# PSUM banks of an attention stage: one ring of seven, or four for row maxima and three for scores, with the maximum unit ahead of the scores on TensorE

## The chip, the cores and the metric

The program runs on one core of a Trainium2 chip. The metric is the device time of one execution in microseconds (us), the median of several. A core has TensorE (matrix products, which land in PSUM), VectorE (DVE in the profile), ScalarE (ACT), GpSimd (POOL) and SyncE (SP), each with its own instruction stream, tied together by semaphores. PSUM has eight banks of 128 x 512 fp32.

## The reference

The input x is 4 x 1024 x 128. Three sublayers are added to it: half a mixture of experts, attention, and half the same mixture again.

```python
x = x + 0.5 * _L0_ffn_ref(_layernorm(x, axis=-1), ...)   # 8 experts, top 2, 128 -> 512 -> 128
x = x + _L0_attn_ref(_layernorm(x, axis=-1), W_qkv, W_o)
x = x + 0.5 * _L0_ffn_ref(_layernorm(x, axis=-1), ...)

# attention: B, N, F, H = 4, 1024, 128, 16; DH = 8; queries, keys and values are one projection
qkv = (x @ W_qkv.T).reshape(b, n, H, DH).transpose(0, 2, 1, 3)
score = softmax(einsum('bhif,bhjf->bhij', qkv, qkv) / SQRT_D, axis=-1)
attn = einsum('bhij,bhjf->bihf', score, qkv)
out = attn.reshape(b, n, F) @ W_o.T
```

The softmax subtracts each row's own maximum, so every score is needed twice: once for the maximum, once for the exponential.

## The kernel before

The stages follow each other: routing, the experts of the first mixture, attention, the experts of the second, the last sums. The change touches attention alone.

Attention works on teams of four heads (NTEAM = 16 teams over four batches), each in two halves of 512 queries. Two kinds of products are made of the same operands:

- **Maximum units.** Unit n is two matmuls side by side in the array (rows 0 to 61 and 64 to 125), each 128 queries x 512 keys, into two PSUM banks (`tensor_row_max`, lines 2247 and 2248). VectorE reduces both banks to row maxima (`vector_row_max`): in one instruction over 1024 elements where the banks are neighbours (line 1970), in two over 512 where the ring wraps (line 1975). There are 512 units. When 16 are done, a "place" chore carries the maxima into the operands of the score products.
- **Score slots.** A slot is one matmul, 128 keys x 512 queries, into one bank; slots come in pairs (`tensor_scores`, lines 2264 and 2268), again side by side. ScalarE takes the exponential of each bank into `att_probs` (line 1456). There are 1024 slots, so 512 pairs. Four slots (two pairs) are a unit for the value products.

After each pair from the third on TensorE runs four value products (`tensor_values`, line 2286) of the unit before: part 0 with the first pair of a unit, part 1 with the second. Part 0 waits until ScalarE has emptied the last slot of that earlier unit, which is the second slot of the pair just before:

```python
if part == 0:
    ...
    TE.wait_ge(*att_bank.emptied(("score", UNIT * (n + 1) - 1)))
```

Below, a pair whose values are part 0 is called an **even pair**, one with part 1 an **odd pair**. For each half-team a "finish" chore copies the value bank out (line 1471) and turns it back through PSUM (line 2309), and further chores (prepare, rows, route) do the layernorm and projection of the next batch and the routing of the last mixture. They are handed out to fixed slots by the list `chores`, and stand behind the value products on each engine.

Everything in attention but the value bank shares seven PSUM banks. `Ring` deals them out in one order, that of the `plan` calls: the pair's two scores, its maximum unit, its chores. What takes a bank waits for whoever held it seven places earlier. TensorE takes its instructions in the order of the program: scores, maximum unit, values, chores. The first 26 maximum units (MAX_FIRST) are run before the first scores, so the unit beside pair k is number k + 26, and the last 26 pairs have none.

Of the kernel before, what the change touches and what calls it, by code (L numbers as in the profile page):

```python
# [9 lines left out]
ALU = mybir.AluOpType  # L10
ACT = mybir.ActivationFunctionType
AX = mybir.AxisListType


class Tally:


    def __init__(self, sem):
        self.sem, self.value = sem, 0
# [35 lines left out]
class Ring:  # L55
# [1 line left out]

    def __init__(self, banks, filled, by_act, maxed, reduced):  # L60
        self.banks = banks
        self.filled, self.by_act, self.maxed, self.reduced = filled, by_act, maxed, reduced
        self.at, self.number, self.holders = {}, {}, []
        self.count = {1: 0, 2: 0}
# [6 lines left out]
        self.number[name] = (size, self.count[size])  # L71

    def bank(self, name, k=0):
        return (self.at[name] + k) % self.banks

    def full(self, name):
        size, n = self.number[name]
# [13 lines left out]
def build_macaron(nc, x, w_qkv, w_o, ln_g, ln_b, router_w, eg, eb, w1, b1, w2, b2, wo, bo, out):  # L91
# [69 lines left out]
    PAIR = 2  # L161
# [15 lines left out]
    V, G, S, TE, Q = nc.vector, nc.gpsimd, nc.scalar, nc.tensor, nc.sync  # L177

    stack = ExitStack()
    with stack:  # L180
# [3 lines left out]
        def semaphore(name):  # L184
            return stack.enter_context(nc.semaphore(name))
# [46 lines left out]
        class RouteSet:  # L232


            def __init__(self, k, owner):
                def buf(name, shape, dt=F32):
                    return sbuf(f"{name}{k}", shape, dt, owner)

                self.stats = buf("stats", [P, BT, 6])
                self.mean_var = buf("mean_var", [P, BT, 2])  # L240
                self.shifted = buf("shifted", [P, BT])
                self.rstd = buf("rstd", [P, BT])
                self.xf = buf("xf", [P, BT, F])
                self.xf_t = buf("xf_t", [P, N])
                self.rows = buf("rows", [P, BT, TOPK, ROW])
                self.logits = buf("logits", [P, BT, E])
                self.others = buf("others", [P, BT, E])
                self.equal = buf("equal", [P, BT, E])
                self.foremost = buf("foremost", [P, BT])
                self.is_top = buf("is_top", [P, TOPK, BT, E])  # L250
                self.picked = buf("picked", [P, TOPK, BT, E])
                self.top = buf("top", [P, TOPK, BT])
                self.ratio = buf("ratio", [P, BT])
                self.chosen = buf("chosen", [P, BT, E], BF16)
                self.tallies = buf("tallies", [P, 2, E, BT + 1])
                self.counts = buf("counts", [P, E, BT + 1])
                self.place = buf("place", [P, BT, E])
                self.place_f = buf("place_f", [P, TOPK, BT])
                self.place_i = buf("place_i", [P, TOPK, BT], I32)
                self.by_dve = semaphore(f"route_dve{k}")  # L260
                self.by_pool = semaphore(f"route_pool{k}")
                self.by_act = semaphore(f"route_act{k}")
                self.rows_out = [semaphore(f"rows_out{k}_{j}") for j in range(TOPK)]
# [7 lines left out]
        psum = stack.enter_context(nc.psum_tensor("psum", [P, 8, 512], F32))  # L271
        bank = [psum[:, i, :] for i in range(8)]
# [5 lines left out]
        first = ExitStack()  # L278
# [26 lines left out]
        class Mixture:  # L305


            def __init__(self, k, beside):
                mixing = ExitStack()
                if beside:  # L310
# [138 lines left out]

        route_bank = [Banks([bank[b]], semaphore(f"route_full{b}"), semaphore(f"route_emptied{b}"))  # L450
                      for b in range(B)]
        att_bank = Ring(7, semaphore("bank_full"), semaphore("bank_emptied"), maxed, reduced)


        side_bank = Banks([value_bank], semaphore("side_full"), semaphore("side_emptied"))
# [134 lines left out]

        def max_banks(n):

            return [att_bank.bank(("max", n), k) for k in range(PAIR)]

        PLACINGS = 2 * NTEAM

# [165 lines left out]


        for n in range(MAX_FIRST):
            att_bank.plan(("max", n), 2)
            if n == HALF_UNITS + 1:
                for chore in first_chores:
                    plan_banks(*chore)
        for slot in range(0, NSCORES, 2):
            att_bank.plan(("score", slot))  # L770
            att_bank.plan(("score", slot + 1))
            for n in max_units(slot + 1):
                att_bank.plan(("max", n), 2)
            for chore in chores[slot] + chores[slot + 1]:
                plan_banks(*chore)
        for slot in HEAD + TAIL:
# [1187 lines left out]
        def vector_row_max(n):  # L1964
            i, g, p, t, keys = max_of(n)
            h = 2 * i + g
            V.wait_ge(maxed, n + 1)
            low, high = max_banks(n)
            if high == low + 1:
                last = V.tensor_reduce(out=neg_part[:, h % 2, keys, p::PAIR, t], in_=psum[:, low:high + 1, :],  # L1970
                                       axis=AX.X, op=ALU.max, negate=True)
            else:

                for k, where in enumerate((low, high)):
                    last = V.tensor_reduce(out=neg_part[:, h % 2, keys, PAIR * k + p, t:t + 1], in_=bank[where],  # L1975
                                           axis=AX.X, op=ALU.max, negate=True)
            last.then_inc(reduced, 1)
            if n % HALF_UNITS == HALF_UNITS - 1:
                V.wait_ge(reduced, n + 1)
                if h >= 2:  # L1980
                    V.wait_ge(*att_bank.full(("place", h - 2)))
                V.tensor_tensor(neg_max[:, h % 2, :], neg_part[:, h % 2, 0, :, :].rearrange("p j t -> p (j t)"),
                                neg_part[:, h % 2, 1, :, :].rearrange("p j t -> p (j t)"),
                                ALU.min).then_inc(max_whole, 1)
# [229 lines left out]
        def tensor_attention():  # L2214
            TE.wait_ge(weighed, BLOCKS)
            TE.wait_ge(combined, HC * BLOCKS)
            TE.wait_ge(turn_copied, BLOCKS)
            for n in range(MAX_FIRST):
                tensor_row_max(n)
                if n == HALF_UNITS + 1:  # L2220
                    for chore in first_chores:
                        tensor_chore(*chore)
            for slot in range(0, NSCORES, 2):
                tensor_scores(slot)
                for n in max_units(slot + 1):
                    tensor_row_max(n)
                if slot >= UNIT:
                    tensor_values(slot // UNIT - 1, slot % UNIT // 2)
                for chore in chores[slot] + chores[slot + 1]:
                    tensor_chore(*chore)  # L2230
            for part in range(2):
                tensor_values(NSCORES // UNIT - 1, part)

        def tensor_row_max(n):
            i, g, p, t, keys = max_of(n)
            s = i % OPERANDS
            if n == i * 2 * HALF_UNITS:
                if i < OPERANDS:
                    TE.wait_ge(max_rows_set, i + 1)
                TE.wait_ge(lefts_in[s], lefts_before(i))  # L2240
                TE.wait_ge(rights_in[s], rights_before(i))
            for emptied in att_bank.empty_before(("max", n)):
                TE.wait_ge(*emptied)
            low, high = max_banks(n)
            q = slice((g * HT + t) * P, (g * HT + t + 1) * P)
            k = slice(keys * HALF, (keys + 1) * HALF)
            TE.matmul(bank[low], left[s][PRODUCTS[0], p, q], right[s][PRODUCTS[0], p, k], start=True, stop=True)  # L2247
            TE.matmul(bank[high], left[s][PRODUCTS[1], p, q], right[s][PRODUCTS[1], p, k],  # L2248
                      start=True, stop=True).then_inc(maxed, 1)

        def tensor_scores(slot):

            i, at = divmod(slot, TURN)
            u, j = divmod(at, UNIT)
            half, kt = divmod(u, BT)
            s, p = i % OPERANDS, j // 2
            if kt == 0 and j == 0:
                TE.wait_ge(max_in[s], 16 * 2 * (placed_before(2 * i + half) + 1))
            low, high = ring_bank(("score", slot)), ring_bank(("score", slot + 1))
            k = slice(kt * P, (kt + 1) * P)  # L2260
            q = slice(half * HALF, (half + 1) * HALF)
            for emptied in att_bank.empty_before(("score", slot)):
                TE.wait_ge(*emptied)
            TE.matmul(low, left[s][WITH_MAX[0], p, k], right[s][WITH_MAX[0], p, q],  # L2264
                      start=True, stop=True).then_inc(att_bank.filled, 1)
            for emptied in att_bank.empty_before(("score", slot + 1)):
                TE.wait_ge(*emptied)
            TE.matmul(high, left[s][WITH_MAX[1], p, k], right[s][WITH_MAX[1], p, q],  # L2268
                      start=True, stop=True).then_inc(att_bank.filled, 1)
# [120 lines left out]
```

## Time and profile before

| | |
|---|---|
| time, median of 3 runs | 1316.57 us (1316.5 to 1319.73) |
| the profiled execution: time, span | 1308.1 us, 1306.4 us |
| scores, from the first to the last exponential | 364 to 1060 us |
| TensorE, VectorE, ScalarE busy, of the span | 88%, 86%, 68% |
| mean granted TensorE clock | 0.978 |

The busy share of TensorE comes from modelled ends of pipelined matmuls, so starts are the better reading: the distance from one start to the next is the pace. Exponentials and reductions overlap their neighbours by about 0.1 us, so a mean duration is longer than the step from one to the next.

### The profile page before, as it was taken

To read this page: it belongs to the slowest core of one execution; us is meant where nothing else is said; L and a number is where in the kernel's file an instruction comes from. 1 tells how busy PE (TensorE), PEld (TensorE's weight loads), DVE (VectorE), ACT (ScalarE), POOL (GpSimd) and SP (SyncE) were. 2 spreads that over 40 slices of the span, in tenths; PEclk is the share of its full clock that TensorE was granted. 3 is DMA by queue.
4 is the path that set the end of the run, shared out by engine and by line. 5 is a ranking of instruction groups with operands and counts; after the bars stand their busy time and mean duration, and the time that the engine had idled before them with its cause. 6 is when DMAs were issued, how large, how long until landed. Compare 5 with 4: busy or idle time off the path is not lost.

```text
span 1306.4 us, 27214 instructions
## 1 busy us (share of the span) xinstructions
PE 1150.1 (88%) x9031; PEld 630.4 (48%) x9031; DVE 1126.8 (86%) x2337; ACT 887.6 (68%) x1879; POOL 482.2 (37%) x545
## 2 busy tenths in 40 slices
PE   3847999888589999999999999999998889999993
PEld 2746888777123223223323223233322258788882
DVE  7877888877899999989998999999999368988885
ACT  1223555555168999898888888898887965455651
POOL 3873547334113000324235313333333117543232
PEclk9999999999679999999999999999999999999997
DMA  8124665564010200002001010001000503554654
GB/s 277 50 70 171 215 212 187 206 215 134 29 50 19 67 6 15 18 18 63 5 27 37 11 32 19 18 26 28 18 5 24 181 31 138 191 204 181 247 199 139
DMA packets 58617, 123.55 MB, mean 95 GB/s; under 512 B 12352, under 2 KB 33826, under 8 KB 58448
## 3 DMA queue, kind: packets, MB, share of 16 engines
q1 hardware_dynamic: 49488, 103.83, 23.1%
q0 software_dynamic: 8704, 16.93, 4.1%
q8 instruction: 75, 1.23, 0.4%
q10 hardware_dynamic: 288, 1.05, 0.2%
q14 instruction: 62, 0.51, 0.1%
HBM read 36.66 MB, written 23.88 MB: 46 GB/s over the span
## 4 chain that ended last, share of the span: by engine, by line
PE 56%; DVE 25%; issue 5%; POOL 5%; ACT 5%; DMA 3%; SPq 1%; DVEq 0%; POOLq 0%; ACTq 0%
PE psum L2286 14%; DVE att_neg_part L1970 12%; PE psum L2264 8%; PE psum L2200 8%; PE psum L2188 7%; PE psum L2190 7%; PE psum L2247 5%; POOL rows_dram L1263 4%; DVE att_neg_part L1975 2%; DMA ffn_block_rows<-rows_dram 2%; DVE ffn_x2c L1911 2%; DVE stats L1604 2%; ACT att_probs L1456 2%; DVE ffn_hidden L1922 1%; PE psum L2309 1%
## 5 line engine op out<-in xcount | busy, mean ns | idle before, releaser
L1456 ACT ACTIVATE att_probs<-psum 128x512 f32<-128x512 f32 x1024 | 554.9, 599 | 59.3 <-PE psum L2268 31.2
L1970 DVE TENSOR_REDUCE att_neg_part<-psum 128x2 f32<-128x1024 f32 x443 | 519.1, 1216 | 33.3 <-PE psum L2248 31.6
L2286 PE MATMUL psum<-att_probs,att_values 128*16 128x256 f32 x4096 | 322.1, 386 | 12.4 <-ACT att_o_t L1471 7.7
L1424 ACT ACTIVATE ffn_silu<-ffn_x2c,ffn_rec 128x256 f32<-128x256 f32 (+1 forms) x320 | 154.6, 487 | 170.1 <-DVE ffn_x2c L1911 170.0
L1279 POOL DMA_INDIRECT y_dram<-ffn_y,ffn_block_rows x144 | 142.4, 989 | 235.0 <-ACT ffn_y L1442 206.5
L2268 PE MATMUL psum<-att_right,att_left 64*128 64x512 f16 x512 | 199.5, 390 | 17.3 <-DVE att_neg_part L1970 13.2
L2247 PE MATMUL psum<-att_right,att_left 62*128 62x512 f16 x512 | 198.4, 388 | 15.6 <-DVE att_neg_part L1970 10.1
L2264 PE MATMUL psum<-att_right,att_left 64*128 64x512 f16 x512 | 199.5, 390 | 8.5 <-DVE att_neg_part L1970 6.8
L2248 PE MATMUL psum<-att_right,att_left 62*128 62x512 f16 x512 | 200.0, 391 | 0.0
L1911 DVE TENSOR_SCALAR ffn_x2c<-psum,ffn_rec 128x256 f32<-128x256 f32 (+1 forms) x320 | 162.8, 513 | 36.7 <-PE psum L2190 33.0
L2188 PE MATMUL psum<-ffn_block_t,ffn_rec 128*128 128x256 f32 (+1 forms) x640 | 179.0, 362 | 1.2 <-ACT ffn_block_t L1375 1.2
L2190 PE MATMUL psum<-ffn_block_t,ffn_rec 128*128 128x256 f32 (+1 forms) x640 | 178.2, 360 | 0.0
L1263 POOL DMA_INDIRECT rows_dram<-rows,place_i x128 | 127.5, 996 | 122.6 <-PE psum L2268 53.6
L2286 PEld LDWEIGHTS psum<-att_probs,att_values 128*16 128x16 f32 x4096 | 69.4, 94 | 192.7 <-issue 134.6
L1922 DVE SCALAR_TENSOR_TENSOR ffn_hidden<-psum,ffn_rec,ffn_silu 128x256 f32<-128x256 f32 (+1 forms) x320 | 144.4, 451 | 19.0 <-ACT ffn_silu L1424 17.0
L2200 PE MATMUL psum<-ffn_hidden,ffn_rec 128*128 128x256 f32 (+1 forms) x640 | 140.6, 363 | 11.8 <-DVE ffn_hidden L1930 11.6
L2264 PEld LDWEIGHTS psum<-att_right,att_left 64*128 64x128 f16 x512 | 47.3, 92 | 203.7 <-ACT att_probs L1456 128.6
L2200 PEld LDWEIGHTS psum<-ffn_hidden,ffn_rec 128*128 128x128 f32 x640 | 111.0, 190 | 32.4 <-DVE ffn_hidden L1930 19.8
L2190 PEld LDWEIGHTS psum<-ffn_block_t,ffn_rec 128*128 128x128 f32 x640 | 117.6, 192 | 13.6
L2188 PEld LDWEIGHTS psum<-ffn_block_t,ffn_rec 128*128 128x128 f32 x640 | 111.9, 192 | 12.2 <-ACT ffn_block_t L1375 1.8
L1192 POOL TENSOR_TENSOR att_attn<-att_o_t,att_inv_sum 128x128 f32<-128x128 f32 x30 | 12.1, 404 | 227.7 <-DVE att_inv_sum L1999 213.0
L1975 DVE TENSOR_REDUCE att_neg_part<-psum 128x1 f32<-128x512 f32 x138 | 88.3, 681 | 4.3 <-PE psum L2248 3.6
(238 smaller groups left out, 1176.6 us busy)
## 6 DMA issues: line engine op xcount, KB each, us to landing
ffn_rec<-record SPq DMA_DIRECT2D x80, 776.5 KB, 3.9
ffn_block_rows<-rows_dram SPq DMA_DIRECT2D x64, 130.0 KB, 3.1
record<-in_L_ffn_W SPq DMA_DIRECT2D x16, 256.0 KB, 6.5
att_left<-q_parts_dram SPq DMA_DIRECT2D x64, 64.0 KB, 2.2
y_dram<-ffn_y,ffn_block_rows POOLq DMA_INDIRECT x144
x_sb<-in_L_attn_x SPq DMA_DIRECT2D x4, 512.0 KB, 7.0
record<-in_L_ffn_Wo SPq DMA_DIRECT2D x8, 256.0 KB, 7.2
rows_dram<-rows,place_i POOLq DMA_INDIRECT x128, 2.4
```

The lines of the kernel that those rows point to most:

```text
L1263: G.indirect_dma_start(rows_dram[k_ffn][:, :], bass.IndirectOffsetOnAxis(ap=r.place_i[:, k, t:t + 1], axis=0), r.rows[:, t, k, :], None).t ...
L1456: S.activation(probs[:, slot % PROBS, :], ring_bank(("score", slot))[:, :], ACT.Exp, scale=unlift).then_inc(att_bank.by_act, 1)
L1911: V.tensor_scalar(mix[k].x2c[:, n % 2, few], chunk_bank[n % 4][:, few], mix[k].rec[:, s, CLIP_LO + c:CLIP_LO + c + 1], mix[k].rec[:, s, CL ...
L1970: last = V.tensor_reduce(out=neg_part[:, h % 2, keys, p::PAIR, t], in_=psum[:, low:high + 1, :], axis=AX.X, op=ALU.max, negate=True)
L2188: TE.matmul(both[:, few], mix[k].rec[:, s, W2 + c * P:W2 + (c + 1) * P], mix[k].block_t[:, m % 2, few], start=True, stop=True)
L2190: TE.matmul(both[:, w1_few], mix[k].rec[:, s, W1 + c * P:W1 + (c + 1) * P], mix[k].block_t[:, m % 2, few], start=True, stop=True).then_inc ...
L2200: last = TE.matmul(y_bank[n % 2][:, few], mix[k].rec[:, s, WO + c * F:WO + (c + 1) * F], mix[k].hidden[:, n % 2, c, few], start=(c == 0), ...
L2247: TE.matmul(bank[low], left[s][PRODUCTS[0], p, q], right[s][PRODUCTS[0], p, k], start=True, stop=True)
L2248: TE.matmul(bank[high], left[s][PRODUCTS[1], p, q], right[s][PRODUCTS[1], p, k], start=True, stop=True).then_inc(maxed, 1)
L2264: TE.matmul(low, left[s][WITH_MAX[0], p, k], right[s][WITH_MAX[0], p, q], start=True, stop=True).then_inc(att_bank.filled, 1)
L2268: TE.matmul(high, left[s][WITH_MAX[1], p, k], right[s][WITH_MAX[1], p, q], start=True, stop=True).then_inc(att_bank.filled, 1)
L2286: last = TE.matmul(value_bank[head * VS:head * VS + VW, q], values[:, b % 2, kt, team * TEAM + head, :], probs[:, (UNIT * n + j) % PROBS, ...
```

## The change

The ring is parted. Maximum units get a ring of their own of banks 0 to 3 (`max_bank`, two units deep), scores and chores one of banks 4 to 6. The units' two banks are now always neighbours, so the branch with two reductions goes. And TensorE writes a pair's maximum unit before its two scores. ScalarE's program is the same.

```diff
-        att_bank = Ring(7, semaphore("bank_full"), semaphore("bank_emptied"), maxed, reduced)
+        MAX_BANKS = 2 * PAIR
+        max_bank = Ring(0, MAX_BANKS, None, None, maxed, reduced)
+        att_bank = Ring(MAX_BANKS, 7 - MAX_BANKS, semaphore("bank_full"), semaphore("bank_emptied"), None, None)
...
             low, high = max_banks(n)
-            if high == low + 1:
-                last = V.tensor_reduce(out=neg_part[:, h % 2, keys, p::PAIR, t], in_=psum[:, low:high + 1, :],
-                                       axis=AX.X, op=ALU.max, negate=True)
-            else:
-
-                for k, where in enumerate((low, high)):
-                    last = V.tensor_reduce(out=neg_part[:, h % 2, keys, PAIR * k + p, t:t + 1], in_=bank[where],
-                                           axis=AX.X, op=ALU.max, negate=True)
-            last.then_inc(reduced, 1)
+            V.tensor_reduce(out=neg_part[:, h % 2, keys, p::PAIR, t], in_=psum[:, low:high + 1, :],
+                            axis=AX.X, op=ALU.max, negate=True).then_inc(reduced, 1)
...
             for slot in range(0, NSCORES, 2):
-                tensor_scores(slot)
                 for n in max_units(slot + 1):
                     tensor_row_max(n)
+                tensor_scores(slot)
                 if slot >= UNIT:
                     tensor_values(slot // UNIT - 1, slot % UNIT // 2)
...
-            for emptied in att_bank.empty_before(("max", n)):
+            for emptied in max_bank.empty_before(("max", n)):
                 TE.wait_ge(*emptied)
```

TensorE's program before, two pairs in a stretch without chores, the even one first (lines 2264 and 2268 are the scores, 2247 and 2248 the maximum unit, 2286 the values; bank_emptied is counted up by ScalarE, row_max_reduced by VectorE):

```order
L2264 MATMUL psum<-att_right,att_left 128x512 [waits bank_emptied]
L2268 MATMUL psum<-att_right,att_left 128x512 [waits row_max_reduced]
L2247 MATMUL psum<-att_right,att_left 128x512 [waits bank_emptied,row_max_reduced]
L2248 MATMUL psum<-att_right,att_left 128x512
L2286 MATMUL psum<-att_probs,att_values 16x256 [waits bank_emptied]
L2286 MATMUL psum<-att_probs,att_values 16x256 x3
L2264 MATMUL psum<-att_right,att_left 128x512 [waits bank_emptied]
L2268 MATMUL psum<-att_right,att_left 128x512 [waits row_max_reduced]
L2247 MATMUL psum<-att_right,att_left 128x512 [waits bank_emptied,row_max_reduced]
L2248 MATMUL psum<-att_right,att_left 128x512
L2286 MATMUL psum<-att_probs,att_values 16x256 x4
```

The same two pairs on TensorE in the changed kernel (lines 2242 and 2243 are now the maximum unit, 2259 and 2263 the scores, 2281 the values):

```order
L2242 MATMUL psum<-att_right,att_left 128x512 [waits row_max_reduced]
L2243 MATMUL psum<-att_right,att_left 128x512
L2259 MATMUL psum<-att_right,att_left 128x512 [waits bank_emptied]
L2263 MATMUL psum<-att_right,att_left 128x512 [waits bank_emptied]
L2281 MATMUL psum<-att_probs,att_values 16x256 [waits bank_emptied]
L2281 MATMUL psum<-att_probs,att_values 16x256 x3
L2242 MATMUL psum<-att_right,att_left 128x512 [waits row_max_reduced]
L2243 MATMUL psum<-att_right,att_left 128x512
L2259 MATMUL psum<-att_right,att_left 128x512 [waits bank_emptied]
L2263 MATMUL psum<-att_right,att_left 128x512 [waits bank_emptied]
L2281 MATMUL psum<-att_probs,att_values 16x256 x4
```

The unit has moved from behind the scores to ahead of them, and so from ahead of the values' wait of its own pair to behind the values of the pair before. The second score's bank was VectorE's before and is ScalarE's now; the maximum unit no longer waits for ScalarE.

## Rows read from the trace of the kernel before

**Rows 1.** The page's head and its first part, busy time and share of the span.

```profile
span 1306.4 us, 27214 instructions
PE 1150.1 (88%) x9031; PEld 630.4 (48%) x9031; DVE 1126.8 (86%) x2337; ACT 887.6 (68%) x1879; POOL 482.2 (37%) x545
```

**Rows 2.** Busy time by stretch: length, then each engine's, granted clock, DMA.

```profile
364.00:1024.00 660.00, 623.82 (x6176) 199.87 (x6175) 619.68 (x874) 580.88 (x1137) 200.97 (x230) 0.99 0.09 24
450.43:469.53 19.10, 18.72 (x202) 5.48 (x198) 18.61 (x22) 18.38 (x37) 0.83 (x2) 1.00 0.11 30
639.59:662.87 23.28, 20.91 (x204) 6.59 (x201) 22.83 (x40) 19.30 (x38) 12.12 (x11) 1.00 0.01 2
1029.70:1038.60 8.90, 6.92 (x80) 1.93 (x80) 0.00 (x0) 8.32 (x17) 0.00 (x0) 1.00 0.58 210
```

**Rows 3.** The page's costliest groups: count, busy time, mean ns, idle before.

```profile
L1456 ACT ACTIVATE att_probs<-psum 128x512 f32<-128x512 f32 x1024 | 554.9, 599 | 59.3 <-PE psum L2268 31.2
L1970 DVE TENSOR_REDUCE att_neg_part<-psum 128x2 f32<-128x1024 f32 x443 | 519.1, 1216 | 33.3 <-PE psum L2248 31.6
...
L1975 DVE TENSOR_REDUCE att_neg_part<-psum 128x1 f32<-128x512 f32 x138 | 88.3, 681 | 4.3 <-PE psum L2248 3.6
```

**Rows 4.** Order of time, 462 to 466 us: start, length, engine, line, count.

```profile
461.44 3.48 DVE L1970 TENSOR_REDUCE att_neg_part<-psum 128x2 f32<-128x1024 f32 x3
...
461.76 0.39 PE L2264 MATMUL psum<-att_right,att_left 64*128 64x512 f16 x1
...
461.99 0.38 PE L2247 MATMUL psum<-att_right,att_left 62*128 62x512 f16 x1
...
462.30 0.62 PE L2286 MATMUL psum<-att_probs,att_values 128*16 128x256 f32 x8
...
462.86 0.39 PE L2264 MATMUL psum<-att_right,att_left 64*128 64x512 f16 x1
...
463.41 0.62 PE L2286 MATMUL psum<-att_probs,att_values 128*16 128x256 f32 x8
...
463.97 0.39 PE L2264 MATMUL psum<-att_right,att_left 64*128 64x512 f16 x1
...
464.83 1.28 DVE L1975 TENSOR_REDUCE att_neg_part<-psum 128x1 f32<-128x512 f32 x2
...
466.02 1.22 DVE L1970 TENSOR_REDUCE att_neg_part<-psum 128x2 f32<-128x1024 f32 x1
```

**Rows 5.** Order of time, 641 to 643 us: one pair and its exponentials.

```profile
641.59 0.39 PE L2264 MATMUL psum<-att_right,att_left 64*128 64x512 f16 x1
...
642.01 1.09 ACT L1456 ACTIVATE att_probs<-psum 128x512 f32<-128x512 f32 x2 [0.49 <-PE psum L2268]
```

**Rows 6.** Order of time, 1032 to 1034 us, where no maximum units are left.

```profile
1031.95 0.39 PE L2264 MATMUL psum<-att_right,att_left 64*128 64x512 f16 x1
...
1032.83 0.39 PE L2264 MATMUL psum<-att_right,att_left 64*128 64x512 f16 x1
...
1033.61 0.63 PE L2286 MATMUL psum<-att_probs,att_values 128*16 128x256 f32 x8 [0.39 <-ACT att_probs L1456]
1034.16 0.39 PE L2264 MATMUL psum<-att_right,att_left 64*128 64x512 f16 x1
```

**Rows 7.** Who waited for whom, 364 to 1024 us: total, times, longest.

```profile
PEld psum L2286 <- ACT att_probs L1456: 42.3, 105, 0.8
PEld psum L2268 <- DVE att_neg_part L1970: 26.3, 38, 1.0
...
DVE att_neg_part L1970 <- PE psum L2248: 29.9, 51, 1.1
...
PE psum L2286 <- ACT att_o_t L1471: 6.9, 20, 0.5
```

**Rows 8.** Order of time, 459 to 461 us, around a place chore.

```profile
459.23 0.39 PE L2264 MATMUL psum<-att_right,att_left 64*128 64x512 f16 x1
...
460.53 0.39 PE L2264 MATMUL psum<-att_right,att_left 64*128 64x512 f16 x1
```

More of the change, by code:

```diff
@@ L55, with __init__ @@
 class Ring:
-    def __init__(self, banks, filled, by_act, maxed, reduced):
-        self.banks = banks
+    def __init__(self, first, banks, filled, by_act, maxed, reduced):
+        self.first, self.banks = first, banks
         self.filled, self.by_act, self.maxed, self.reduced = filled, by_act, maxed, reduced
@@ L73, in bank @@
     def bank(self, name, k=0):
-        return (self.at[name] + k) % self.banks
+        return self.first + (self.at[name] + k) % self.banks
     def full(self, name):
@@ L591, in max_banks @@
         def max_banks(n):
-            return [att_bank.bank(("max", n), k) for k in range(PAIR)]
+            return [max_bank.bank(("max", n), k) for k in range(PAIR)]
         PLACINGS = 2 * NTEAM
@@ L764, in build_macaron @@
         for n in range(MAX_FIRST):
-            att_bank.plan(("max", n), 2)
+            max_bank.plan(("max", n), 2)
             if n == HALF_UNITS + 1:
@@ L772, in build_macaron @@
             for n in max_units(slot + 1):
-                att_bank.plan(("max", n), 2)
+                max_bank.plan(("max", n), 2)
             for chore in chores[slot] + chores[slot + 1]:
```

## The prediction

> **What bounds the kernel now.** The page first: 1306.4 us of span, TensorE 88% busy, VectorE 86% [rows 1]. Neither is full, and the change touches attention alone, so the view to go by is the busy time by stretch. From the first scores at 364 us to the last maximum unit at 1024 us, 660 us, TensorE is busy 623.8 us, VectorE 619.7 and ScalarE 580.9 [rows 2]: three engines within a tenth of each other. A stretch of sixteen pairs with only the regular chores takes 19.1 us and VectorE is busy 18.6 of it; one with routing work on VectorE takes 23.3 and VectorE is busy 22.8 [rows 2]. By busy time VectorE looks like the bound.
>
> The order of time says what sets the pace inside a pair. In the light stretch scores start at 461.76, 462.86, 463.97: 1.10 and 1.11 us, so 2.21 for two pairs. Within a pair the maximum unit follows the scores by 0.23 us and the values the unit by 0.31 [rows 4]. The pair at 462.86 is an even one: its values start at 463.41, and the next scores 0.56 us later. From the scores of the odd pair before (461.76) to these values it is 1.65 us. Where that comes from: the exponentials start 0.42 us after their scores, two of them take 1.09 us [rows 5], which makes 1.51, and 0.14 is left for the semaphore and the weight load. So the values of an even pair start as soon as the last exponential of the pair before allows: the 1.65 is a chain over two engines, and the reader should see that it hardly has slack, since on TensorE's own work alone they could have started at 1.10 + 0.23 + 0.31 = 1.64.
>
> The tail proves that it is a chain. There no maximum units are left, TensorE has 0.23 us less to do in every pair, and still two pairs take 1034.16 - 1031.95 = 2.21 us: the values again stand 1.66 us behind the odd pair's scores, and TensorE idles 0.39 us before them, released by the exponential [rows 6]. So the loop (odd scores, two exponentials, even values, next odd scores) is 1.65 + 0.56 = 2.21 us with or without the units; before the change they lie in its hole.
>
> VectorE's own step: three reductions in 3.48 us with the last 1.22 long, so (3.48 - 1.22) / 2 = 1.13 us a unit, and 1.19 for a wrapped one (464.83 to 466.02) [rows 4]. Two units are 2.26: VectorE is a shade slower than the 2.21 loop, falls behind, and catches up when TensorE does a chore.
>
> **The unit ahead of the scores.** It runs as many matmuls as before. What counts is on which side of the values' wait they stand. Take the odd pair's scores as time 0. Its values start at 0.31; the next unit at 0.87, the even pair's scores at 1.10. On TensorE's work alone its values could start at 1.10 + 0.31 = 1.41, no longer 1.64, but the exponential releases them at 1.65 as before. TensorE idles 0.24 us, with the next unit queued behind the wait. After the values come 0.56 us, now the next maximum unit, 0.23 us, and only then the odd scores: 1.65 + 0.56 + 0.23 = 2.44 us for two pairs. The unit of the odd pair has moved out of the hole and into the loop, at its full 0.226 us (461.99 - 461.76 for the same kind of pair of matmuls). The trace doesn't show a unit directly behind values; scores behind values take 0.56, and I take the same.
>
> How often that is paid. At most in each even pair that has both values and a unit, 2 to 484, so 242 of them: 242 x 0.226 = 54.7 us, the upper end. It isn't paid where a chore of TensorE or a delay by VectorE already makes the even values come later than the exponential. The waits tell: in these 660 us the values' weight loads were released by an exponential 105 times [rows 7], and those have no slack to give. 105 x 0.226 = 23.7. Where VectorE sets the pace in such pairs two of them took 2.26 before and 2.44 after, a loss of 0.18 instead; with about half of them so, 105 x 0.20 = **21.0**. Besides, the even values wait 20 times for the copy of the value bank by ScalarE [rows 7]. That copy too is a chain from the odd scores, with the next unit behind the wait: 20 x 0.226 = **4.5**.
>
> **Three banks for scores and chores.** Scores alone: the second score now waits for the exponential of the first score of the pair before, whose end is 0.42 + 0.60 = 1.02 behind its matmul, with 0.07 for the semaphore (an estimate, half of the 0.14 above) 1.09; the next pair isn't due before 1.10. It fits with nothing to spare. A place chore takes one of the three banks: then the second score of the next pair waits for the second exponential of the last, 1.51 + 0.07 = 1.58, while its scores were due at 460.53 - 459.23 = 1.30 [rows 8]. Its values then start at 1.58 + 0.31 = 1.89 and the next odd scores at 1.89 + 0.56 + 0.23 = 2.68; before they came at 461.76 - 459.23 = 2.53 [rows 4, 8]. 0.15 us, in about half of the 31 place chores (the others stand beside VectorE's chores): **2.2**. A finish chore occupies TensorE longer and its bank is ready by then: 0.
>
> **Four banks for maxima.** A unit waits for the reduction two before, as it in effect did. 138 single reductions, 69 wrapped units [rows 3], become 69 joined ones: 0.06 us each by the step, 4.1 us of VectorE's time, which is worth something only where VectorE sets the pace: **-1**, between 0 and -4.
>
> **What VectorE gains.** Slower loops let it run up to its two units of lead, where it was behind before; its routing chores start from there. That is up to some 0.4 us for each run of such chores; about a dozen runs in three batches, some of which had the lead already: **-4**, between 0 and -10. In stretches like 639.59 to 662.87, 1.46 us a pair with VectorE busy for 98% [rows 2], the loop of 1.22 a pair is hidden, and nothing is lost.
>
> **The last 26 pairs** have no unit; their loop needs no more than three banks: 0. The first 26 units, without scores, save a few wraps: 0.
>
> **The sum.** 21.0 + 4.5 + 2.2 - 1 - 4 = 22.7 us. The profiled execution would go from 1308.1 to 1330.8; its own time lies 8.5 us below the median of the runs shown, and the difference is carried over: 1316.6 + 22.7 = 1339.
>
> **The rivals.**
>
> *Faster: VectorE is the bound.* VectorE waits 29.9 us in 51 places for the unit's matmul [rows 7]; with units written first and never tied to ScalarE it would always have one ready, and the wraps give 4.1 more. If half the waits went: 1316.6 - 15 - 4 = about 1298. The Trainium skill speaks for it (Perfetto Trace Analysis, Identifying the Most-Contended Engine): the engine with the highest occupancy is the one to relieve, and here that is VectorE. Against it stands the tail, where VectorE does nothing and the pace is the same 2.21. It decides if the even values' wait has slack after all, of 0.2 us or more in most pairs; the trace shows 0.39 us of idling in the tail and none behind it. Chance 0.08.
>
> *No change.* VectorE's chores absorb nearly all, the loop is as long as its work: 1313 to 1320. For it: VectorE's reductions already hold up the second scores' weight loads in 38 places, 26.3 us in all [rows 7], and 19.1 us for sixteen pairs is 1.19 a pair [rows 2], close to 1.22. Against it: the 1.19 already holds the chores, which come on top of 1.22 too. Chance 0.06.
>
> *Slower by twice as much.* Chores squeeze the three banks harder than I worked out, and all 242 even pairs lose: 1316.6 + 54.7 = 1371. Against it: where VectorE had made values late there is slack of more than 0.226. Chance 0.10.
>
> *The clock.* The Trainium skill (TensorE: Matmul & The Clock Gate, A second HAM failure mode) tells of a kernel whose clock fell between bursts when it cycled through PSUM. What the trace has to say: from 1029.70 to 1038.60 TensorE idles 0.39 us in every 2.2, busy 6.92 of 8.90 us, and the granted clock is 1.00, the level of 2.4 GHz [rows 2]. The gap that I forecast is shorter. If it fell to 1.2 GHz, a pair would take about twice its 1.10 us, beyond 1500 us in all. Chance 0.01.
>
> **How the numbers follow.** The forecast has 0.75. A measurement of this kernel tells about 0.3%, 4 us, from no change. Faster 0.08, same 0.06, slower 0.86. The range leaves out the faster case and the top of the doubled one: 1320 (4 us of net loss: full credits, half of the 105 waits absorbed) to 1362 (+45).
>
> **What would show it.** Two pairs without chores at 2.44 us by the scores' starts, not 2.21; TensorE idle for 0.24 us before the even values, released by the exponential, far over 105 times; reductions 512, all joined, VectorE's idle time up by 15 us or more and released by TensorE; the tail unchanged at 2.21; clock 1.00. If two pairs come out at 2.26, the loop is wrong and VectorE is the bound. If the second scores wait often for exponentials apart from place chores, the three banks are the cost and not the order. What would make me wrong is a shorter way from score to exponential once the banks are parted, which no row shows.

## The result and the profile after

The changed kernel is slower: 1338.0 us (1337.65 to 1339.51) against 1318.15 us (1316.5 to 1320.85) before, 1.0153 times as long, with a 95% interval of 1.0129 to 1.0177. Timed again beside the experiments it took 1324.77 us against 1307.23: 1.0136 (1.0116 to 1.0157). That is 19.9 and 17.5 us more. Forecast were 22.7 us, within 1320 to 1362.

The page of the changed kernel, its head, busy times and costliest groups that answer to [rows 1, 3] (line 1971 is now the reduction, 1458 the exponential, 2281 the values, 2242 and 2243 the maximum unit, 2259 and 2263 the scores):

```profile
span 1335.9 us, 26640 instructions
PE 1148.6 (86%) x9031; PEld 620.1 (46%) x9031; DVE 1127.5 (84%) x2268; ACT 889.4 (67%) x1879; POOL 481.6 (36%) x545
...
L1971 DVE TENSOR_REDUCE att_neg_part<-psum 128x2 f32<-128x1024 f32 x512 | 601.0, 1215 | 51.5 <-PE psum L2243 44.6
L1458 ACT ACTIVATE att_probs<-psum 128x512 f32<-128x512 f32 x1024 | 555.2, 596 | 83.1 <-PE psum L2263 75.9
...
L2242 PE MATMUL psum<-att_right,att_left 62*128 62x512 f16 x512 | 204.1, 399 | 44.6 <-DVE att_neg_part L1971 41.8
```

No engine has more than 2 us more to do. The reductions are 512 joined ones, and their busy time fell from 519.1 + 88.3 to 601.0 us, 6.4 less. What grew is waiting: 51.5 us before the reductions where it was 33.3 + 4.3, and 83.1 us before the exponentials where it was 59.3.

The order of time in a light stretch, TensorE's scores, units and values (rows that answer to [rows 4]):

```profile
476.86 0.39 PE L2242 MATMUL psum<-att_right,att_left 62*128 62x512 f16 x1
...
477.09 0.38 PE L2259 MATMUL psum<-att_right,att_left 64*128 64x512 f16 x1
...
477.63 0.62 PE L2281 MATMUL psum<-att_probs,att_values 128*16 128x256 f32 x8 [0.17 <-ACT att_probs L1458]
...
478.19 0.39 PE L2242 MATMUL psum<-att_right,att_left 62*128 62x512 f16 x1
...
478.42 0.38 PE L2259 MATMUL psum<-att_right,att_left 64*128 64x512 f16 x1
...
478.73 0.62 PE L2281 MATMUL psum<-att_probs,att_values 128*16 128x256 f32 x8
...
479.29 0.39 PE L2242 MATMUL psum<-att_right,att_left 62*128 62x512 f16 x1
...
479.51 0.38 PE L2259 MATMUL psum<-att_right,att_left 64*128 64x512 f16 x1
```

This is the chain of the prediction, read off. Even scores at 477.09; their values at 477.63, 0.54 behind and not 0.31, released by the exponential; then 0.56 us to the next unit (478.19), 0.23 to the odd scores (478.42), and 1.09 to the next even ones (479.51). Two pairs take 2.42 us; before they took 2.21, forecast was 2.44.

Busy time by stretch, the same pairs as in [rows 2], sixteen light ones and sixteen with routing work on VectorE:

```profile
461.51:481.94 20.43, 18.99 (x200) 5.38 (x198) 19.05 (x19) 18.51 (x37) 0.83 (x2) 1.00 0.10 28
658.56:681.37 22.81, 19.44 (x201) 5.40 (x199) 22.36 (x37) 18.73 (x37) 12.20 (x11) 1.00 0.01 2
```

The light ones went from 19.10 to 20.43 us, VectorE's share from 97% to 93%. The clock is 1.00. The loaded ones went the other way, from 23.28 to 22.81.

Who waited for whom in attention (total, times, longest), answering to [rows 7]; PEld is TensorE's weight load, PE its matmul:

```profile
PEld psum L2281 <- ACT att_probs L1458: 48.5, 91, 0.9
...
PE psum L2242 <- DVE att_neg_part L1971: 33.3, 52, 1.1
PE psum L2281 <- ACT att_probs L1458: 15.5, 92, 0.2
PE psum L2281 <- ACT att_o_t L1473: 13.6, 24, 0.6
...
DVE att_neg_part L1971 <- PE psum L2243: 42.8, 68, 1.4
```

The values' weight loads wait for an exponential about as often as before (91 times, before 105). What is new is the row of the matmuls: they stand still 92 times for an exponential, where before the same view (364 to 1024 us) has no such wait, since the units filled the hole. For the copy of the value bank they wait 24 times, 13.6 us, and before 20 times, 6.9 us.

By stages, taken from the starts and ends in the traces, the profiled execution of before (1308.1 us) against the changed kernel's beside the experiments (1324.58 us): the 486 pairs that have a unit took 660.6 and 674.0 us; the units ahead of the first scores 28.1 and 30.1 (with one unit more in it, since a unit now precedes the first scores); the tail 35.8 and 35.6. So attention as a whole is 15.2 us longer. The profiled execution that belongs to the result agrees (673.9 us for the pairs, 15.1 us for attention). But it begins attention at 344.8 us, where before began at 335.5, and takes 251.6 us behind it, where before took 246.4, although those stages have the same program. That is why the two profiled spans differ by 29.5 us. The medians differ by 19.9, since the profiled execution of before lay 10.0 us under the median of 1318.15. The traces thus show some 15 us of the change in attention; what the medians show above that, 2 to 5 us, isn't seen there, and its cause is open.

### The profile page after: what moved, and what is told of

Its sections match the earlier page's. It is cut to its first block, busy times and chain, and to the rows that moved or that the text cites. A ratio compares the mean times of both kernels' runs of the same rounds, so it can differ in the third digit from the quotient of the medians.

```text
span 1335.9 us, 26640 instructions
## 1 busy us (share of the span) xinstructions
PE 1148.6 (86%) x9031; PEld 620.1 (46%) x9031; DVE 1127.5 (84%) x2268; ACT 889.4 (67%) x1879; POOL 481.6 (36%) x545
## 4 chain that ended last, share of the span: by engine, by line
PE 52%; DVE 25%; ACT 11%; issue 7%; DMA 2%; POOL 1%; SPq 1%; another core or an unknown queue 0%; DVEq 0%; POOLq 0%; ACTq 0%
PE psum L2281 12%; DVE att_neg_part L1971 10%; ACT att_probs L1458 8%; PE psum L2195 7%; PE psum L2242 7%; PE psum L2183 7%; PE psum L2185 7%; PE psum L2259 5%; DVE stats L1606 2%; DVE ffn_x2c L1913 2%; DMA ffn_block_rows<-rows_dram 1%; PE psum L2304 1%; DVE ffn_hidden L1924 1%; ACT att_o_t L1473 1%; PE psum L2263 1%
## 5 line engine op out<-in xcount | busy, mean ns | idle before, releaser
L1971 DVE TENSOR_REDUCE att_neg_part<-psum 128x2 f32<-128x1024 f32 x512 | 601.0, 1215 | 51.5 <-PE psum L2243 44.6
L1458 ACT ACTIVATE att_probs<-psum 128x512 f32<-128x512 f32 x1024 | 555.2, 596 | 83.1 <-PE psum L2263 75.9
L2281 PE MATMUL psum<-att_probs,att_values 128*16 128x256 f32 x4096 | 322.2, 386 | 33.3 <-ACT att_probs L1458 17.0
L2242 PE MATMUL psum<-att_right,att_left 62*128 62x512 f16 x512 | 204.1, 399 | 44.6 <-DVE att_neg_part L1971 41.8
L2243 PE MATMUL psum<-att_right,att_left 62*128 62x512 f16 x512 | 204.2, 399 | 0.0
L2263 PE MATMUL psum<-att_right,att_left 64*128 64x512 f16 x512 | 195.4, 382 | 0.3
L2259 PE MATMUL psum<-att_right,att_left 64*128 64x512 f16 x512 | 195.1, 381 | 0.0
L2242 PEld LDWEIGHTS psum<-att_right,att_left 62*128 62x128 f16 x512 | 47.4, 93 | 247.7 <-DVE att_neg_part L1971 141.8
L2195 PE MATMUL psum<-ffn_hidden,ffn_rec 128*128 128x256 f32 (+1 forms) x640 | 143.9, 369 | 13.5 <-DVE ffn_hidden L1932 10.5
L2185 PEld LDWEIGHTS psum<-ffn_block_t,ffn_rec 128*128 128x128 f32 x640 | 118.2, 193 | 13.6
```

Of the source, the lines that this page charges most:

```text
L1458: S.activation(probs[:, slot % PROBS, :], ring_bank(("score", slot))[:, :], ACT.Exp, scale=unlift).then_inc(att_bank.by_act, 1)
L2185: TE.matmul(both[:, w1_few], mix[k].rec[:, s, W1 + c * P:W1 + (c + 1) * P], mix[k].block_t[:, m % 2, few], start=True, stop=True).then_inc ...
L2195: last = TE.matmul(y_bank[n % 2][:, few], mix[k].rec[:, s, WO + c * F:WO + (c + 1) * F], mix[k].hidden[:, n % 2, c, few], start=(c == 0), ...
L2281: last = TE.matmul(value_bank[head * VS:head * VS + VW, q], values[:, b % 2, kt, team * TEAM + head, :], probs[:, (UNIT * n + j) % PROBS, ...
```

## The experiments

Each is timed against the kernel before on the same chip: the first four on one chip (before 1306.95 us), the next four on a second (1307.23), the last on a third (1307.9). The first four expectations were written when before stood at 1318.15 us; their bounds in absolute times are better read as distances from it. "Sixteen" is the time of sixteen light pairs, from score to score: 19.10 us before.

**The rings parted, the order of before.** From the changed kernel:

```diff
+                tensor_scores(slot)
                 for n in max_units(slot + 1):
                     tensor_row_max(n)
-                tensor_scores(slot)
```

> The PSUM ring is parted in four and three, the order on TensorE stays that of before (scores, maximum unit, values). Theory (the loss is the unit's place behind the values' wait, in the loop odd scores - exponentials - even values - odd scores): the loop keeps its 2.21 us for two pairs; against it stand 69 wrapped reductions less (0.06 us each, where VectorE paces) and a second score that waits for ScalarE after a place chore (about 0.27 us, some 16 times). Within 5 us of the kernel before. Rival (three banks for scores and chores are the cost): most of the 20 us is here already, 1333 or more. Rival (VectorE is the bound and the order is indifferent): faster than before by 4 us or more and the changed kernel's loss unexplained.

1308.56 us, 1.0008 (0.9994 to 1.0022). Sixteen 19.25 us, two pairs 2.21:

```profile
461.62 0.39 PE L2259 MATMUL psum<-att_right,att_left 64*128 64x512 f16 x1
...
462.73 0.39 PE L2259 MATMUL psum<-att_right,att_left 64*128 64x512 f16 x1
...
463.83 0.39 PE L2259 MATMUL psum<-att_right,att_left 64*128 64x512 f16 x1
```

So neither the three banks nor the joined reductions are the loss. VectorE's shorter work brings nothing that can be measured, though a small gain and the place chores' cost could cancel here. The 0.15 us more in sixteen stand at the place chore, where the second score came 0.26 us behind the first, and after a finish chore (0.15).

**The order alone, one ring of seven.** In the kernel before, with the `plan` calls in the same new order:

```diff
             for slot in range(0, NSCORES, 2):
-                tensor_scores(slot)
                 for n in max_units(slot + 1):
                     tensor_row_max(n)
+                tensor_scores(slot)
```

> One ring of seven as before, but each pair's maximum unit is dealt its banks and written ahead of its scores. Theory: the unit is in the loop, as in the changed kernel; besides, seven places back from the second score now stands the unit of the pair just before, so that score waits for VectorE's newest reduction and VectorE has no lead. A chain from the end of one reduction over score, values, unit, two reductions: 0.06 + 0.31 + 0.56 + 0.42 + 1.22 = 2.57 us for two pairs, over the 2.44 of the changed kernel. Slower than the changed kernel, 1345 to 1370. Rival (the banks are the cost and the order is free): 1318.

1366.05 us, 1.0454 (1.0434 to 1.0475), 59 us over before; the range that was given, taken from 1318.15, meant 27 to 52. Two pairs take 478.86 - 476.27 = 2.59 us, 2.57 forecast:

```profile
476.27 0.38 PE L2264 MATMUL psum<-att_right,att_left 64*128 64x512 f16 x1
...
477.40 0.38 PE L2264 MATMUL psum<-att_right,att_left 64*128 64x512 f16 x1
477.76 0.39 PE L2268 MATMUL psum<-att_right,att_left 64*128 64x512 f16 x1
478.07 0.63 PE L2286 MATMUL psum<-att_probs,att_values 128*16 128x256 f32 x8
...
478.86 0.38 PE L2264 MATMUL psum<-att_right,att_left 64*128 64x512 f16 x1
```

The second score (477.76) comes 0.36 us behind the first (477.40). The first exponential of the pair before had ended 0.48 us earlier; VectorE's newest reduction ended at 477.70, and that is what it waits for. With the unit first, one ring is much worse than two. The parting rescues some 41 us of a loss that the order makes.

**The unit first in the even pairs only.**

```diff
+                if slot // 2 % 2 != 0:
+                    tensor_scores(slot)
                 for n in max_units(slot + 1):
                     tensor_row_max(n)
-                tensor_scores(slot)
+                if slot // 2 % 2 == 0:
+                    tensor_scores(slot)
```

> The changed kernel's two rings; the maximum unit stands ahead of the scores only in the even pairs (values part 0) and behind them in the odd pairs. Theory: between the even values and the odd scores nothing is added, and between the odd scores and the even values there is room, so two pairs take 2.21 us: the same time as with the rings alone, within 4 us, and about 18 us less than the changed kernel. Rival (what costs is having units ahead of scores at all, through later exponentials or a fuller ring): half of the 20 us, about 1328.

1321.73 us, 1.0113 (1.0093 to 1.0133). The expectation fell: two pairs take 2.38 us and not 2.21. At 15 us over before it lies nearer to the rival, half of the changed kernel's loss through a fuller ring.

```profile
464.09 0.38 PE L2262 MATMUL psum<-att_right,att_left 64*128 64x512 f16 x1
...
464.40 0.62 PE L2284 MATMUL psum<-att_probs,att_values 128*16 128x256 f32 x8
464.50 2.06 ACT L1458 ACTIVATE att_probs<-psum 128x512 f32<-128x512 f32 x4 [0.32 <-PE psum L2266]
...
464.95 0.39 PE L2262 MATMUL psum<-att_right,att_left 64*128 64x512 f16 x1
...
465.15 0.39 PE L2266 MATMUL psum<-att_right,att_left 64*128 64x512 f16 x1
...
465.69 0.62 PE L2284 MATMUL psum<-att_probs,att_values 128*16 128x256 f32 x8
...
466.47 0.38 PE L2262 MATMUL psum<-att_right,att_left 64*128 64x512 f16 x1
```

The even values stand right behind their scores (0.31), so the values' wait is indeed out of the way. But the odd pair's first score now comes only 0.86 us behind the even one, and its second (465.15) 1.06 behind: it waits for the bank that the even pair's first exponential empties (started at 464.50, ended at 465.10). From there TensorE has a unit, the values, another unit: 1.32 us to the next even scores. 1.06 + 1.32 = 2.38. With three banks the second score of a pair didn't come closer than 1.06 to 1.07 us to the scores before it; where the units are bunched, that closes a second loop. I had left that out. No run has a fourth bank for the scores, so this cause is read from the trace and not tested by itself.

**The unit first in the odd pairs only.** The same edit with the parity changed.

> The changed kernel's two rings; the maximum unit stands ahead of the scores only in the odd pairs. Theory: this is the one unit that lies between the even values and the odd scores, so two pairs take 2.44 us and the whole loss of the changed kernel is here: 1334 to 1340. Rival (units ahead of scores cost alike wherever they stand): half of the 20 us, about 1328.

1334.53 us, 1.0209 (1.0188 to 1.0231), 27.6 us over before. It lies within 1334 to 1340 only because before is 11 us lower on this chip: that range meant 16 to 22 us over 1318.15, the changed kernel's loss, and it is more. 684.7 us go to the pairs with units, against the changed kernel's 674.0. Two light pairs take 472.93 - 470.50 = 2.43 us, as in the changed kernel:

```profile
470.50 0.39 PE L2262 MATMUL psum<-att_right,att_left 64*128 64x512 f16 x1
470.70 0.39 PE L2266 MATMUL psum<-att_right,att_left 64*128 64x512 f16 x1
...
471.27 0.63 PE L2284 MATMUL psum<-att_probs,att_values 128*16 128x256 f32 x8
471.83 0.39 PE L2245 MATMUL psum<-att_right,att_left 62*128 62x512 f16 x1
...
472.06 0.38 PE L2262 MATMUL psum<-att_right,att_left 64*128 64x512 f16 x1
...
472.93 0.39 PE L2262 MATMUL psum<-att_right,att_left 64*128 64x512 f16 x1
```

A unit lies between even values and odd scores (471.83), and the values start 0.14 us after their exponential's end, so the loop is closed as in the changed kernel. But it isn't alone: the even scores follow the odd ones by 0.87 us here, so their second score (470.70) waits for a bank as in the last run. By that wait alone the values could have started at 471.23 instead of 471.27 (an estimate from the steps of this row), and two pairs would take 2.39. This run can't tell the two loops apart; the changed kernel against the first run, and the run with two units below, can. What comes on top is at the chores: sixteen take 20.75 us, not 20.43, with the second score 0.48 us late behind the place chore, where the changed kernel has 0.25.

**The changed kernel itself.**

> The changed kernel itself, to have it on the same chip as the others. From the stretches of its trace (pairs with a unit 673.9 us against 660.6, the first units 30.1 against 28.1) and stages before and after that the change doesn't touch at their times of before: 1.012 times the kernel before.

1324.77 us, 1.0136 (1.0116 to 1.0157); the pairs with units 674.0 us, sixteen 20.4.

**Two units ahead of the odd pair's scores, none in the even pair.**

```diff
-                for n in max_units(slot + 1):
-                    tensor_row_max(n)
+                if slot // 2 % 2:
+                    for n in (*max_units(slot - 1), *max_units(slot + 1)):
+                        tensor_row_max(n)
                 tensor_scores(slot)
```

> The changed kernel's rings; both maximum units of two pairs stand ahead of the odd pair's scores, the even pair has none. A dose of two where the changed kernel has one. Theory (a unit between the even values and the odd scores adds its 0.226 us to a loop of 2.21): two light pairs take 2.21 + 0.45 = 2.66 us, sixteen with their chores some 22.2 us, the whole 1340 to 1355 if before is 1307. Rival (what counts is how many pairs have the unit ahead of their scores, half as many here): at or under the changed kernel's time.

1370.22 us, 1.0499 (1.0474 to 1.0523). Two pairs take 2.64 us (476.99 to 479.63), sixteen 22.13:

```profile
476.99 0.38 PE L2260 MATMUL psum<-att_right,att_left 64*128 64x512 f16 x1
...
478.63 0.62 PE L2282 MATMUL psum<-att_probs,att_values 128*16 128x256 f32 x8 [0.19 <-ACT att_probs L1458]
479.19 0.39 PE L2243 MATMUL psum<-att_right,att_left 62*128 62x512 f16 x1
...
479.42 0.38 PE L2243 MATMUL psum<-att_right,att_left 62*128 62x512 f16 x1
...
479.63 0.38 PE L2260 MATMUL psum<-att_right,att_left 64*128 64x512 f16 x1
```

So none, one and two units between the even values and the odd scores make 2.21, 2.43 and 2.64 us for two pairs: 0.22 for each. The whole is 15 us over the range that I expected; over before, the pairs with units take 60.1 us more with two units there and 13.4 with one. The scores are bunched here as in the fourth run, which had 10.7 us on top of the changed kernel; that, and a larger dose being covered by fewer chores, may be the excess, but no run took it apart.

**Late values.** In the changed kernel the value products come one pair later; `att_probs` gets ten banks, not eight, and the finish chore stands two slots later.

```diff
-    PROBS = 2 * TEAM
+    PROBS = 2 * TEAM + 2
...
-                if slot >= UNIT:
-                    tensor_values(slot // UNIT - 1, slot % UNIT // 2)
+                if slot >= UNIT + 2:
+                    tensor_values((slot - 2) // UNIT - 1, (slot - 2) % UNIT // 2)
...
-                    if slot >= PROBS and slot % UNIT == 0:
-                        S.wait_ge(valued, slot // UNIT - PROBS // UNIT + 1)
+                    if slot >= PROBS and slot % 2 == 0:
+                        S.wait_ge(valued, (slot - PROBS) // UNIT + 1)
...
-                for k, wait in enumerate((3, 5, 7) if last else (3, 6, 9)):
+                for k, wait in enumerate((5, 6, 7) if last else (5, 8, 11)):
```

> The changed kernel with the value products one pair later (part 0 with the odd pair, part 1 with the next even pair), so that no value product waits for the pair just before; two more banks of att_probs in SBUF pay for it, and the finish chores stand two slots later. The units stay ahead of the scores, and the rings stay. Theory: with the loop open only the engines' own steps are left, TensorE 1.095 a pair, VectorE 1.13: two light pairs take 2.19 to 2.26 us, and the loss of the changed kernel is gone or nearly: 1300 to 1312 if before is 1307. Rival (the three banks or the units' place cost by themselves): it stays within 5 us of the changed kernel.

1305.46 us, 0.9982 (0.9970 to 0.9994). The loss is gone, with the units still ahead of the scores and the rings parted. Sixteen take 19.24 us, and the values stand 0.31 us behind the scores, with no wait; in all pairs with units, none of those that need the last exponential of a unit starts less than 1.0 us after its end:

```profile
469.24 0.38 PE L2260 MATMUL psum<-att_right,att_left 64*128 64x512 f16 x1
...
469.55 0.62 PE L2282 MATMUL psum<-att_probs,att_values 128*16 128x256 f32 x8
...
470.33 0.38 PE L2260 MATMUL psum<-att_right,att_left 64*128 64x512 f16 x1
...
471.43 0.38 PE L2260 MATMUL psum<-att_right,att_left 64*128 64x512 f16 x1
```

2.19 us for two pairs is TensorE's own steps: 0.22 from unit to scores, 0.31 to the values, 0.56 to the next unit, 1.09 a pair.

**Late values, scores first.** The same with the order of before.

> As the last, but with the scores ahead of the unit as before the change (rings parted). Theory: with the loop open the order hardly matters: within 4 us of the last run, and no faster than before by more than 6 us, since VectorE's 1.13 us a unit is next. Rival (the order costs in itself): faster than the last run by 13 us or more.

1306.1 us, 0.9994 (0.9983 to 1.0004), within 1 us of the last. With the loop open the order doesn't matter: 0.6 us, where with early values it made 16 (the changed kernel against the first run). Ten banks and later chores by themselves bring little: with the order of before it is 0.9994 with them and 1.0008 without (the first run).

**Late values, the unit first in the even pairs only.** The third run's order on the seventh.

> The units ahead of the scores in the even pairs alone, as in the third run, with the late values of the seventh, so that no value product waits for the pair just before. It asks what made the third run 1.1% slower. Theory formed from its trace (with three banks the odd pair's second score waits for the even pair's first exponential, 1.07 us after the even scores, and from there TensorE has two units, the scores and the values to do, 1.32 us, before the next even scores): the values have no part in it, two light pairs still take 2.38 us, sixteen about 20.0, and the time stays 10 us or more above before. Rival (the values' wait was behind the third run's loss too): 2.26 us or less for two pairs and the time of the kernel before.

1330.3 us, 1.0177 (1.0153 to 1.0201). Two pairs take 471.44 - 469.06 = 2.38 us, the third run's figure to the hundredth, although no value starts less than 1.2 us after its exponential's end:

```profile
469.06 0.38 PE L2263 MATMUL psum<-att_right,att_left 64*128 64x512 f16 x1
...
470.13 0.39 PE L2267 MATMUL psum<-att_right,att_left 64*128 64x512 f16 x1
...
471.44 0.38 PE L2263 MATMUL psum<-att_right,att_left 64*128 64x512 f16 x1
```

The second loop therefore doesn't run through the values; what is left of it is the wait of the second score (470.13) for its bank. Why this one is 8 us slower than the third run in all is open. Part of it is in the light stretches already: sixteen take 20.24 us against 20.03, with the finish chores two slots later.

## Why the prediction was right

**The loop.** Right in its place and in its size: 2.44 forecast, 2.42 to 2.43 in the changed kernel; 2.21 with no unit in it, 2.64 with two, and 2.19 with the loop opened. That the late values bring the time back with rings and order as changed, and that with them the order is indifferent, shows that the wait of the even values is the cause, not an accompaniment.

**How often it is paid.** This is the term that was mis-sized, and the total hides it. Take from the traces of before and of the changed kernel (beside the experiments), for each of the 242 even pairs, the time from the odd scores before it to the odd scores behind it:

| even pairs, as they stood before | pairs | longer by, us |
|---|---|---|
| values start within 0.16 us of their exponential's end | 78 | 15.4 |
| values wait for the copy of the value bank | 20 | 4.2 |
| all others | 144 | -4.8 |
| together | 242 | 14.8 |

Each of the first 98 lost 0.20 us on average, as the prediction has it, and the copy's term (4.5) was right. But the 105 waits were not the pairs without slack. Only 46 of the 78 are among them. Fifteen are the same pairs as fifteen of the 20 copies, and so were counted twice. In the other 44 the values started 0.19 to 1.4 us after their exponential's end; they had slack, and together they became 1.4 us shorter. The prediction's "those have no slack to give" is the step that failed: the view names what came last before a weight load, and the distance from the releaser's end to the start tells whether there was slack. That 32 pairs which it leaves out make up for most of this is luck. So is part of the closeness of 1338.0 to the forecast 1339: the sum was of attention, where 22.7 us were forecast and 15 are seen, and the medians' other 2 to 5 us lie outside it.

By stretches it is the same: of the 29 sixteens between pair 16 and pair 480, 21 became longer, 18.4 us together, and 8 shorter, 3.1 us together, where the terms for the two kinds of wait and the place chores were 27.7. The sign "far over 105 times" was only half met: 112 or 113 even pairs now start within 0.16 us of the exponential's end, 78 before. VectorE's idle time before its reductions went up by 13.9 us, not 15 or more.

**VectorE's gain.** -4 was forecast and the eight shorter sixteens show -3.1. Six of them hold 2.4 us or more of VectorE's chores, two follow directly behind such work. That fits the mechanism (VectorE starts its chores with a lead), but with the rings alone eleven sixteens are shorter too, 2.5 us together, so the order may have little part in it. No run took it apart.

**Three banks.** A place chore was to hold the second score for 0.28 us; it comes 0.25 behind the first in 15 of 30 places, about the half that was assumed, and 0.41 in six more. In the light stretch the pairs around it take 2.65 us, before 2.53; 2.68 was forecast. Over all thirty places these steps are 0.7 us shorter, though, so the +2.2 isn't there as a sum. In the changed kernel from 471.99 to 473.56 us:

```profile
472.21 0.38 PE L2259 MATMUL psum<-att_right,att_left 64*128 64x512 f16 x1
472.46 0.39 PE L2263 MATMUL psum<-att_right,att_left 64*128 64x512 f16 x1
472.78 0.62 PE L2281 MATMUL psum<-att_probs,att_values 128*16 128x256 f32 x8
```

That the three banks "fit with nothing to spare" was truer than I used: in the changed order they hold up little but place chores (21 of the 26 second scores that come over 0.15 us late), in the bunched order of the third run they are the bound.

**Wraps.** -1 was forecast; the rings alone, with all reductions joined, give 1.0008, so it is nothing that can be told, the place chores against it included.

**The rivals.** VectorE as the bound is out: its waits for units went up, from 33.5 us (29.9 for the joined reductions, 3.6 for the wrapped ones) to 42.8, and parting the rings, which leaves it less to do, makes nothing faster. The Trainium skill's rule of the most-contended engine (Perfetto Trace Analysis, Identifying the Most-Contended Engine) would have pointed there; in this trace three engines within a tenth of each other hold one another up, and the bound is the chain. The clock stayed at 1.00 in the light stretches, and the mean of the whole was 0.978 beside the experiments, as before the change (0.974 in the profiled execution of the result). The doubled loss isn't there.

**A version that beats both** is barely there: the late values with the unit first are 0.9982 times before, 2 us, less than the 0.3% that I called telling. TensorE's 2.19 us for two pairs lies too close under the 2.21 of before, and VectorE's 2.26 lies over it.

## What to carry to other kernels

Where an in-order engine feeds a second one and waits for it in the same round, draw the loop and ask of each instruction on which side of the wait it stands: work behind the producer and ahead of the wait lies in the hole and is free, the same work behind the wait is paid in full, here 0.22 us each time. Such a loop shows in the profile as a pace that stays the same where work falls away (the tail without units), and it can be tested by giving the waited-for data one round more. How many rounds it binds is read from the distance between the releaser's end and the start of what it releases, not from a count of waits.

A smaller ring is not measured by whether it fits at the present pace but by the least distance that it allows between rounds; reordering can turn an idle limit into the bound.

## What the runs showed of the hardware

The starts repeat to a hundredth of a us over light stretches: two light pairs took 2.38 us in both kernels that bunch the units, and sixteen pairs 20.43 or 20.44 us in both profiled executions of the changed kernel. The whole time does not: the kernel before had a median of 1318.15 us at the result and 1306.95, 1307.23 and 1307.9 on the three chips of the experiments, 0.8% apart. In the profiled runs of the changed kernel the difference lies outside the pairs: 344.8 against 334.8 us to the start of attention, 673.9 and 674.0 for the pairs, 251.6 against 248.4 behind the last exponential. What makes it is open. The changed kernel's 1324.77 us set against 1318.15 would have shown 6.6 us of the change.

A wait ends at different distances from what releases it: value products started 0.14 us after the end of their exponential (median of the 78 pairs before), scores 0.05 to 0.06 us after the exponential or the reduction that freed their bank (470.70 after 470.64 in the fourth run, 465.15 after 465.10 in the third, 477.76 after 477.70 in the second). The prediction took 0.07 for the latter.
